# Token stage: the exact reciprocal of the deviation against exp(-ln) with a Newton step, and an earlier place for the weight preparation

## What is computed

```python
result = _dw_conv2d(image, t_kern, stride, pad)            # 31x31 template, per channel
m1 = _dw_conv2d(image, mean_kern, stride, pad)             # box mean
m2 = _dw_conv2d(image * image, mean_kern, stride, pad)     # box mean of squares
std = jnp.sqrt(m2 - m1 * m1)
result = result / (std + EPS)                              # EPS = 1e-09
result = result.mean(axis=1)
result = jnp.where(jnp.isnan(result), 0, result)
```

## Time and profile before

| | |
|---|---|
| median of 3 runs | 2167.36 us (2160.34 to 2170.95) |
| profiled execution | 2172.09 us, span 2170.3 us, mean granted TensorE clock 0.918 |
| busy over the span | PE 1915.2 us (88%), DVE 1214.9 (56%), ACT 854.4 (39%), POOL 773.6 (36%) |
| token stage | 0 to 627 us of the span |
| attention stage | to about 1455 us |
| MLP stage | to the end |
| RECIPROCAL of the deviation, line 451 | 12 x 12.95 us on DVE |

### The profile page before, as it was taken

How to read it: one execution, slowest core, us unless ns; L and a number is a source line. 1 busy time by engine, 2 the same in 40 slices (tenths; PEclk the granted TensorE clock), 3 DMA queues, 4 the chain that set the end, 5 groups by cost and what they waited for, 6 DMA issues and landing times. The chain is left out here.

```text
span 2170.3 us, 31220 instructions
## 1 busy us (share of the span) xinstructions
PE 1915.2 (88%) x11768; PEld 1651.7 (76%) x11768; DVE 1214.9 (56%) x1671; ACT 854.4 (39%) x1164; POOL 773.6 (36%) x515
## 2 busy tenths in 40 slices
PE   4788998988948988998899899859999999999997
PEld 4788888888946777777778677748787877877876
DVE  7999999899944564565565554532413314134141
ACT  5553443445234563665355545512222212222121
POOL 3223222122254443554254344414333333243332
PEclk9899999999977898897998898879999999999999
DMA  9122212112101000200100010023000000000000
GB/s 143 71 93 77 108 45 91 71 45 117 59 29 53 21 15 8 79 21 14 67 21 21 8 59 14 21 112 144 20 1 19 19 0 19 0 19 20 1 10 11
DMA packets 32211, 95.87 MB, mean 44 GB/s; under 512 B 18630, under 2 KB 18758, under 8 KB 26569
## 3 DMA queue, kind: packets, MB, share of 16 engines
q1 hardware_dynamic: 31500, 89.80, 13.0%
q10 hardware_dynamic: 576, 4.19, 0.5%
HBM read 81.37 MB, written 24.15 MB: 49 GB/s over the span
## 5 line engine op out<-in xcount | busy, mean ns | idle before, releaser
L554 PE MATMUL conv<-w_hi,x_hi 128*128 128x368 f16 (+5 forms) x1320 | 358.0, 280 | 8.5 <-POOL w_lo L262 4.8
L554 PE MATMUL conv<-w_lo,x_hi 128*128 128x368 f16 (+5 forms) x1320 | 358.5, 280 | 0.0
L554 PE MATMUL conv<-w_hi,x_lo 128*128 128x368 f16 (+5 forms) x1320 | 356.8, 280 | 0.0
L820 POOL TENSOR_TENSOR probs<-probs,mask 128x512 f32<-128x512 f32 x128 | 177.6, 1392 | 299.1 <-ACT probs L894 299.1
L1079 PE MATMUL mixed<-v,probs 128*128 128x65 f32 x1536 | 231.2, 308 | 24.2 <-POOL probs L820 15.0
L1079 PEld LDWEIGHTS mixed<-v,probs 128*128 128x128 f32 x1536 | 214.7, 221 | 41.4 <-POOL probs L820 16.8
L1253 POOL TENSOR_TENSOR ha_lo<-raw_c,ha_hi 128x512 fp32r<-128x512 f32 x128 | 165.0, 1289 | 209.9 <-DVE ha_hi L1303 209.9
L1291 ACT ACTIVATE raw_c<-ring,sh 128x512 f32<-128x512 f32 x128 | 88.1, 688 | 372.7 <-PE ring L1388 372.6
L1388 PE MATMUL ring<-ha_hi,wh 128*128 128x512 f32 x512 | 209.4, 409 | 16.8 <-POOL ha_lo L1253 16.8
L554 PEld LDWEIGHTS conv<-w_hi,x_hi 128*128 128x128 f16 x1320 | 192.9, 146 | 17.6 <-issue 9.5
L1388 PE MATMUL ring<-ha_lo,wh 128*128 128x512 f32 x512 | 206.2, 403 | 0.0
(11 more groups left out here) (144 smaller groups left out, 3929.2 us busy)
## 6 DMA issues: line engine op xcount, KB each, us to landing
xt<-x_columns_in SPq DMA_DIRECT2D x12, 1163.0 KB, 5.2
xp<-x_patches_in SPq DMA_DIRECT2D x12, 1152.0 KB, 5.1
hidden_words<-hidden_weights_in SPq DMA_DIRECT2D x8, 1408.0 KB, 9.2
words<-hidden_words SPq DMA_DIRECT2D x32, 352.0 KB, 3.1
wh<-hidden_words SPq DMA_DIRECT2D x2, 4096.0 KB, 21.3
tokens<-result ACTq DMA_DIRECT2D x4, 1024.0 KB, 5.3
lines<-tokens SPq DMA_DIRECT2D x4, 1024.0 KB, 5.6
h<-tokens SPq DMA_DIRECT2D x4, 1024.0 KB, 7.7
```

The costliest lines, as they stand in the source:

```text
L554: ins = pe.matmul(out, xs[:, c, RI - 1 - i:RI - 1 - i + NR, :, x].rearrange("p r g -> p (r g)"), w, start=(t == 0), stop=(t == len(terms) ...
L820: pool.tensor_tensor(diag, diag, both, ALU.mult).then_inc(s_mask, 1)
```

## The change

1. ACT's `moments` goes on behind Sqrt: `guess = Ln(std + 1e-9)` and `guess = Exp(-guess)`, each over the whole tile, with a semaphore wait ahead of each.
2. DVE's `inverse` replaces line 448 and RECIPROCAL by two `scalar_tensor_tensor` over the tile: `std = (std + eps) * guess`, `rinv = (std - 2) * guess`, which is one Newton step with the sign reversed. It now waits for Exp.
3. `scale` becomes a `scalar_tensor_tensor` with the factor -1/(taps x channels), which takes the sign and the constant that line 448 had.
4. `fold_weights` on DVE moves from between `scale(11, 0)` and `scale(11, 1)` to the end of body 10, behind `inverse(11)`. `split_weights` on POOL moves from behind the second quarter of plane 11 to ahead of the first.
5. A tile for epsilon and its memset are added, and the counts of `s_const` go up by one.

```diff
             pool.memset(sh.neg_half[:], -0.5).then_inc(s_const, 1)
+            pool.memset(eps_t[:], EPS_T).then_inc(s_const, 1)
...
                 if not (last and c == 2):
                     split_lo((c + 1) % CHANNELS, n + 1)
+                else:
+                    split_weights()
...
-                    if last and c == 2 and b == 1:
-                        split_weights()
...
                 act.activation(std[:], std[:], ACT.Sqrt).then_inc(s_std, 1)
+                act.wait_ge(s_std, 3 * n + 1)
+                act.activation(guess[:], std[:], ACT.Ln, bias=eps_t[:]).then_inc(s_std, 1)
+                act.wait_ge(s_std, 3 * n + 2)
+                act.activation(guess[:], guess[:], ACT.Exp, scale=-1.0).then_inc(s_std, 1)
...
-                dve.wait_ge(s_std, n + 1)
-                dve.tensor_scalar(std[:], std[:], EPS_T, float(TAPS * CHANNELS), ALU.add, ALU.mult)\
-                   .then_inc(s_point, 1)
+                dve.wait_ge(s_std, 3 * n + 3)
+                dve.scalar_tensor_tensor(out=std[:], in0=std[:], scalar=EPS_T, in1=guess[:],
+                                         op0=ALU.add, op1=ALU.mult).then_inc(s_point, 1)
                 dve.wait_ge(s_point, n * 3 + 4)
-                dve.reciprocal(rinv[:], std[:]).then_inc(s_point, 1)
+                dve.scalar_tensor_tensor(out=rinv[:], in0=std[:], scalar=2.0, in1=guess[:],
+                                         op0=ALU.subtract, op1=ALU.mult).then_inc(s_point, 1)
...
-                dve.tensor_tensor(part[:, :, cols], got, rinv[:, :, cols], ALU.mult).then_inc(s_part, 1)
+                dve.scalar_tensor_tensor(out=part[:, :, cols], in0=got, scalar=-1.0 / (TAPS * CHANNELS),
+                                         in1=rinv[:, :, cols], op0=ALU.mult, op1=ALU.mult).then_inc(s_part, 1)
...
                 scale(n, 0)
-                if last and c == 2:
-                    fold_weights()
                 scale(n, 1)
...
                     inverse(g2, c2, n + 1)
+                if last and c == 1:
+                    fold_weights()
```

More of the change, by code:

```diff
@@ L103, in token_stage @@
         tstat = sb("tstat", [CHANNELS, 8])
+        eps_t = sb("eps_t", [P, 1])
         w_hi = sb("w_hi", [P, CHANNELS, RI, PR, CJ * PC], F16)
@@ L115, in token_stage @@
         std = sb("std", [P, PR, SIDE])
+        guess = sb("guess", [P, PR, SIDE])
         rinv = sb("rinv", [P, PR, SIDE])
@@ L235, in _ @@
             pool.memset(sh.neg_half[:], -0.5).then_inc(s_const, 1)
-            pool.wait_ge(s_const, 4)
+            pool.memset(eps_t[:], EPS_T).then_inc(s_const, 1)
+            pool.wait_ge(s_const, 5)
             pool.affine_select(out=ident[:], in_=ident[:], compare_op=ALU.not_equal, fill=1.0, base=0,
@@ L351, in first @@
                 bands(0)
-                act.wait_ge(s_const, 4)
+                act.wait_ge(s_const, 5)
                 turned(0)
@@ L405, in _ @@
             dve.wait_ge(s_tdve, 5)
-            dve.wait_ge(s_const, 4)
+            dve.wait_ge(s_const, 5)
             inner = tpad.rearrange("p (r c) -> p r c", c=TCOLS)[:, PR:PR + TH, PC:PC + TH]
@@ L522, in _ @@
             pe.sem_inc(s_conv, 12)
-            pe.wait_ge(s_const, 5)
+            pe.wait_ge(s_const, 6)
             def turn_sums(n, ks):
```

## The result

| | before | after |
|---|---|---|
| median of four runs each (before: the three shown above and one more) | 2165.53 us | 2192.10 us (2185.86 to 2200.52) |
| ratio, 95% interval | | 1.0135 [1.0106, 1.0164] |
| profiled execution: time, span | 2172.1, 2170.3 | 2185.86, 2184.1 |
| DVE busy over the span | 1214.9 | 1150.0 |
| ACT busy | 854.4 | 943.7 |

By the ratio the change costs 1.35%; the two medians lie 1.2% apart. The forecast of 2204 us was 0.5% too high, the sign and the mechanism were right. DVE lost 65 us of busy time, and still the stage that it bounds became 30.5 us longer.

What follows compares the result with a forecast made beforehand. DVE sets the token stage's period, ACT adds 3.6 us, PE follows. Ten bodies +37.4, start +1.5, end -2.5 gave +36.4 us on 2172.1, or 2208.5; with the median 4.7 lower, 2204 us, range 2160 to 2232.

Steps and rivals of the forecast that it cites:

- Removed, 14.8: On DVE in body 1: RECIPROCAL (12.95 us) and line 448 (1.81) go away, together -14.8 us.
- Two steps, 4.5: On DVE in body 1: two added whole-tile steps with two SBUF inputs, 2.23 us each, together +4.5 us.
- Scale, +0.2: On DVE in body 1: `scale` as a three-operand step with one PSUM input, +0.2 us for four.
- Detour, 6.4: Ln, Exp and two table loads on ACT ahead of `xt_sq` lengthen DVE's wait from 1.41 to 7.8 us: +6.4.
- Turns, body 1, 6.4: POOL's two adds and `x_lo`, taking turns with DVE's new steps and `valid`, hold DVE up by +6.4 us.
- Body 0 kind, +2.3: Channel 0 planes, where POOL's two steps are copies: -3.1 + 5.4 = +2.3 us a plane.
- Body 2 kind, +6.6: Channel 2 planes: POOL's `total` and `result` steps, then `x_lo` on the first running sum, +6.6 us a plane.
- Start, +1.5: Plane ahead of the loop, with `inverse` and `x_lo` but no `scale` or adds: -3.1 + 4.6 = +1.5 us.
- end, -2.5: Plane 11, from the last t0 (end of line 443) to POOL's last `result`: -2.5 us, between -7 and 0.
- No turns for whole-tile steps: Faster rival: POOL holds up only running sums, not the two new steps and `valid`; 2148 us, chance 0.12.
- The lines are the limit: No-change rival: if DVE gets ahead, PE's transposes and their lines limit the period; 2160 us, chance 0.10.
- A dearer detour: Slower rival: an ACT table switch costs 2.57 us instead of 1.28, +28 us in 11 planes; 2232 us, chance 0.08.

Runs made afterwards that it cites:

- run 7: Changed kernel with RECIPROCAL and its one-tile step back on DVE; Ln and Exp stay and are waited for, unread: 2244.65 us, ratio 1.0383 against the kernel before.
- run 8: Changed kernel without Ln and Exp on ACT, `guess` a constant 1, the two new DVE steps kept: 2124.34 us, ratio 0.9847 against the kernel before.
- run 1: Changed kernel with Ln and Exp moved on ACT behind the second of four units of `down_m`: 2140.70 us, ratio 0.9905 against the kernel before.
- run 4: Changed kernel with Ln and Exp replaced by two Squares, which need no table loads: 2165.67 us, ratio 1.0008 against the kernel before.
- run 5: Kernel before with only the weight preparation moved to its new places: 2166.67 us, one execution (before: 2161.62).
- run 6: Changed kernel with the weight preparation back at its old places: 2186.13 us, one execution.
- run 2: Changed kernel with POOL's `x_lo` computed for only 128 of 2304 columns: 2164.42 us, ratio 1.0007 against the kernel before.
- run 3: Kernel before with POOL's `x_lo` computed for only 128 of 2304 columns: 2170.77 us, ratio 1.0036 against the kernel before.

## Why the prediction was right, and where it was off

**The bound.** DVE's path sets the period, with its waits for ACT. Right: with 6.5 us added to one wait (run 7) the period grows by 6.5 us, and with ten taken from the steps and 6 given back (run 8) it shrinks by 4.

**Removed, 14.8.** Right: from the start of line 448 to the start of `valid` DVE took 14.72 us, and that stretch is now 6.07 (168.62 to 174.69).

**Two steps, 4.5.** They take 2.29 alone (run 1), together 4.6. **Scale, +0.2.** It was nothing: two take 1.26, as before. The prediction's own rows give +0.2 for two steps (1.48 against 1.29), and so +0.4 for the four of a plane.

**Detour, 6.4.** It was 6.55 by the wait (7.96 against 1.41); Ln takes 2.02, not the 1.92 of Sqrt. The function isn't the reason: in run 4 a Square with the same bias takes 2.02 in its place, and the Square behind it, without a bias, 1.93.

**Turns, body 1, 6.4.** This term was too large: 0.58 and 0.96 for the adds and 4.4 for `x_lo`, 5.95 in all. The order of the turns was as written: `x_lo` between the second new step and `valid`. My price of a turn was POOL's whole duration, 1.3 and 4.61; DVE loses 0.2 to 0.3 less than that each time. The rule of the Trainium skill that I weighed against the rows ("SBUF — State Buffer", section "Who interferes with whom") holds, with 6.69 us for a step of 2.29. Body 1: -14.8 + 4.6 + 6.55 + 5.95 = +2.3, measured +2.4. (The prediction's -3.7 + 6.4 is +2.7, not +2.8. And the periods that it lists as a sign, 50, 50.5 and 52.5 to 53.5, are not those of its sum, which are 50.0, 53.2 and 52.5 by kind; measured 49.4, 52.8 and 51.8.)

**Body 0 kind, +2.3.** It was +1.7. I took 0.7 for the two copies; line 455 takes 2.29 there and line 458 takes 2.58, against 2.29 alone, so they cost 0.3. With scale's 0.2 and the smaller price of `x_lo` that is the miss.

**Body 2 kind, +6.6.** It was 5.9 (6.1, 6.0 and 5.6). The adds cost 1.5, the last `result` 2.54 (I said 2.6), and the 5.4 by which the first running sum was to be late came as 1.19 of waiting for `lines` and 4.05 of standing still.

**Start, +1.5, and end, -2.5.** +1.1 and -2.3. That the start came so near is in part luck: DVE waits there 3.98 us for a DMA, which the prediction doesn't have, and the two halves of the change don't add there. Of the end I had said that moving the weights "gives little by itself"; it takes 1.6 (runs 5 and 6), and the end is shorter because RECIPROCAL is gone from it. Exp, though, was done late enough there to hold DVE: 7.4 us at line 455 in the last plane, which the +8.3 behind t0 of my text implies.

**The sum.** +30.5 in place of +36.4 at the end of the token stage. On the profiled execution the forecast was 2208.5 against 2185.86, 22.6 too high: 5.9 from these terms, 14.6 from the attention stage at another granted clock, 2.2 from the stage behind it (713.1 in place of 715.3 us). Only the first part is a miss of the reasoning. The last two are a thing that one execution can't give.

**The rivals.** *No turns for whole-tile steps* fell with runs 2 and 8. *The lines are the limit* did not arise in the changed kernel (4.6 us in four places), but run 2 meets it. *A dearer detour* fell with run 4.

**What stays open.** Why the attention stage runs at 0.87 and 814 us in one execution and 0.86 and 829 in another. The other profiles lie between (run 6 815.9 us, run 1 819.4, run 8 820.2, run 7 823.3, run 2 823.5, run 5 824.0, run 3 826.3, run 4 828.0), with no relation to their edits that I can show. Nothing was tried on it. Also not tried: the version of run 1 without part 4, which by runs 5 and 6 should be some 1.6 us faster still, and a place for `x_lo` where DVE waits anyway.

## What to carry to other kernels

Before a long instruction is replaced by short ones, look at what the neighbour engine did under it. Here ten us of DVE time a plane were saved by duration, and five to ten of them went back, because POOL's work had lain under the long instruction and now falls on steps that stand still for it. And if the replacement needs another engine first, its place in that engine's order matters more than its length: the same Ln and Exp cost 6.5 us a plane ahead of the work that DVE waits for, and under 3 in the middle of it. That one edit, which also lets POOL's steps fall at better times, turns +1.35% into -1%.

## What the runs showed of the hardware that I had not expected

- **RECIPROCAL is not held up by POOL, and it isn't the only one.** 128x2048 f32 take 12.95 us, to within 2 ns in all twelve planes, with POOL beside it or not, and POOL's 4.61 us step is no slower under it. Nor are the `scale` steps, which read one input from PSUM and one from SBUF: two of them take 1.29 under `x_lo` and without it (run 1). Steps with two inputs in SBUF stand still until the POOL instruction that was ahead of them is over (`valid` 6.69 for 2.29, a running sum 4.75 for 0.70).
- **A short POOL step suffers as much.** 128 columns take 0.43 us under RECIPROCAL (run 3) and 2.49 behind a running DVE step with two inputs in SBUF (run 2). The duration in a row is thus no measure of the work.
- **The token scaling, with one tile as input and a factor per row, is slowed too:** eight take 8.57 us in one order and 12.66 in the other (run 5). So it isn't only steps with two whole tiles as inputs.
- **Ln and Exp in turn cost two loads a plane on DVE's path**, and a load costs 1.283 us and nothing more (run 4).
- **With the same instructions, PE's busy time in one stage differs by 2%** (703.9 and 718.4 us) between the profiled executions of two kernels, at a granted clock that differs by 0.01. A change worth under 15 us should be read from its own stage.
